# A graph network and expert kernel on one core: update, query and final phases fused by tiles

## The reference, cut to what matters

```python
h = layernorm(x) @ Win.T + b_in
for l in range(3):
    Q, K, V = h @ Wq.T + bq, h @ Wk.T + bk, h @ Wv.T + bv        # 4 heads of 64
    scores = einsum('ehd,egd->ehg', Q[src], K[tgt]) / 8
    msg = einsum('ehg,egd->ehd', softmax(scores), V[tgt]) + Ee[type]
    h = relu(layer_norm(h + segment_sum(msg @ Wo.T + bo, src)) * g + b)
x = x + layernorm(x) + relu(h @ W1.T + b1) @ W2.T + b2
z = layernorm(x); router: 8 logits of z, softmax, the best 2
x = x + weighted sum over the 2 experts: gelu(layernorm(z)*g_e + b_e @ W1_e + b1_e) @ W2_e + b2_e
```

## Time and profile before

| | us |
|---|---|
| median of 3 timed runs | 5030.3 (5026.69 to 5033.61) |
| the profiled execution's own time | 4994.96 |
| its span | 4992.9 |
| mean granted clock of PE | 0.896 |
| PE busy | 3540.9 (71%) |
| DVE busy | 2880.3 (58%) |
| POOL busy | 2496.8 (50%) |
| ACT busy | 1974.2 (40%) |

### The profile page before, as it was taken

One profiled execution on the slowest core, in us unless ns is written; L12 is line 12 of the kernel. 1 busy time (PEld: TensorE's weight loads), 2 busy tenths in 40 slices (PEclk: granted clock), 3 DMA queues, 4 the chain that ended last, 5 costly groups with the idle time before them and its releaser, 6 DMA issues.

```text
span 4992.9 us, 105216 instructions
## 1 busy us (share of the span) xinstructions
PE 3540.9 (71%) x32051; PEld 2742.5 (55%) x32052; DVE 2880.3 (58%) x7542; ACT 1974.2 (40%) x6195; POOL 2496.8 (50%) x2694
## 2 busy tenths in 40 slices
PE   4554066777777786777777777777777778629992
PEld 1113045666666644666666654566666665529991
DVE  7777025777677752777777764377777775620001
ACT  0000044444444445444444443544444444204440
POOL 4787705665666630566665642366666662041113
PEclk9998588999999968999999995899999996659996
DMA  1000034555555523555555542455555552515553
GB/s 27 1 1 6 16 106 128 158 159 156 156 161 160 158 64 131 150 158 159 158 159 159 156 127 87 137 158 160 161 159 160 161 157 82 173 68 185 184 179 111
DMA packets 258168, 640.75 MB, mean 128 GB/s; under 512 B 58336, under 2 KB 121325, under 8 KB 250286
## 3 DMA queue, kind: packets, MB, share of 16 engines
q0 software_dynamic: 161280, 480.04, 33.6%
q1 hardware_dynamic: 96830, 160.07, 9.5%
HBM read 589.52 MB, written 51.00 MB: 128 GB/s over the span
## 4 chain that ended last, share of the span: by engine, by line
PE 34%; DMA 21%; issue 18%; DVE 5%; POOL 4%; another core or an unknown queue 2%; SPq 1%; DVEq 1%; POOLq 1%; ACT 1%; ACTq 0%
DMA arena<-kv_d,gidx 19%; PE bank L1252 7%; PE bank L1242 5%; PE bank L1362 4%; PE bank L1229 4%; PE bank L1374 4%; PE bank L1219 3%; POOL arena L493 2%; PE bank L1235 1%; PE bank L1214 1%; DVE arena L750 1%; POOL tok_d L533 1%; DMA xin<-hid_d 1%; PE bank L1292 1%
## 5 line engine op out<-in xcount | busy, mean ns | idle before, releaser
L493 POOL DMA_INDIRECT arena<-kv_d,gidx x1776 | 1750.8, 986 | 1147.7 <-PE bank L1252 660.9
L1242 PEld LDWEIGHTS bank<-qbd,kt_s 128*128 128x128 f32 x7104 | 979.6, 200 | 55.3 <-ACT kt_s L994 26.4
L709 DVE TENSOR_REDUCE sc<-bank 128x32 f32<-128x512 f32 x888 | 613.7, 691 | 664.9 <-remote 363.4
L1242 PE MATMUL bank<-qbd,kt_s 128*128 128x128 f32 x7104 | 974.8, 282 | 26.7 <-ACT kt_s L994 24.4
L1229 PE MATMUL bank<-ident,arena 128*128 128x128 f32 x3552 | 696.8, 290 | 378.5 <-DMA arena<-kv_d,gidx 350.4
L1252 PE MATMUL bank<-att,arena 128*64 128x64 f32 x14208 | 654.0, 232 | 293.4 <-DVE arena L750 250.0
L1252 PEld LDWEIGHTS bank<-att,arena 128*64 128x64 f32 x14208 | 531.8, 140 | 472.7 <-issue 427.8
L994 ACT ACTIVATE kt_s<-bank 128x512 f32<-128x512 f32 x888 | 521.9, 588 | 581.2 <-PE bank L1229 548.9
L1229 PEld LDWEIGHTS bank<-ident,arena 128*128 128x128 f32 x3552 | 420.5, 145 | 539.6 <-DMA arena<-kv_d,gidx 511.9
L733 DVE TENSOR_TENSOR att<-at_s,arena 128x1024 f32<-128x1024 f32 x444 | 549.1, 1237 | 81.4 <-DVE at_s L730 74.6
L471 POOL DMA_INDIRECT rec_d<-arena x391 | 451.3, 1154 | 175.1 <-issue 126.9
(11 more groups left out here) (205 smaller groups left out, 3857.3 us busy)
## 6 DMA issues: line engine op xcount, KB each, us to landing
arena<-in_pack SPq DMA_DIRECT2D x56, 1030.0 KB, 5.1
arena<-kv_d,gidx POOLq DMA_INDIRECT x1776
xin<-hid_d SPq DMA_DIRECT2D x175, 128.0 KB
kv_d<-arena SPq DMA_DIRECT2D x75, 256.0 KB, 2.0
hid_d<-arena SPq DMA_DIRECT2D x100, 128.0 KB
arena<-in_w SPq DMA_DIRECT2D x4, 2048.0 KB, 9.5
y_d<-arena SPq DMA_DIRECT2D x56, 128.0 KB, 3.7
rec_d<-arena POOLq DMA_INDIRECT x391
```

What stands on the lines that cost most here:

```text
L493: pool.indirect_dma_start(kv[:, t // UB, t % UB, :], None, kv_d, bass.IndirectOffsetOnAxis(gidx[:, h, t - h * HT:t - h * HT + 1], 0),).the ...
L709: dve.tensor_reduce(sc[:, p // 2 % 2, 2 * (p % 2):2 * (p % 2) + 2], bank[p % 4][:, :].rearrange("p (t g s h) -> p t g h s", t=2, g=H, s=W) ...
L1242: ins = mm(bk[:, o:o + P], kt_s[:, p % 2, u, c, :], qbd[:, p % 4, u, :], start=False, stop=(c == KC - 1), skip_group_check=True)
```

## The change

Update and query phase of a layer become one stage, `uq_phase`, that goes by single tiles: in step k each engine does the update of tile k, the statistics of tile k-1, the output of tile k-2, the turning of tile k-3, the products of tile k-4 and the writes of tile k-5, written out without a loop. Update and final phase become `uf_phase` in the same way, over 10 steps of depth. The outer loop over the layers is written out too.

The sums now lie by head (`sums`, 64 rows by 4 heads by nodes): the adds of the edge stage write four runs of 16 numbers, and PE takes them as they lie, four products of 64 rows per tile with Wo cut by heads. The counts are read in place. Neither ACT nor POOL touches the sums or the counts any more. The hidden state no longer goes through `hid_d` to be turned: PE turns it out of `hout` (ACT takes the positive part while it copies). The old state is still read from `hid_d`, by tiles and ahead of time.

In the projection ACT also writes x + layernorm(x) (`xb`, five calls per group, each with a `hold`), SP stores it beside the hidden state and waits for it before it loads the next x; the final stage reads it instead of x. The sums' memset ahead of edge stage 0 moves from POOL to DVE, behind the edge bias `eewo` and ahead of the one-hots (L816); the later ones stay with POOL, behind the last product of the update. `eewo` is made at the end of the query part, by four products. `xnb` is made by POOL out of x1. The logits of all tiles get their bias in one instruction.

DVE in the edge stage:

```diff
                     w = dve.snap(wreg[2 * p + u], min_val=0, max_val=NW - 1)
-                    a = acc[:, ds(w, 1), :].squeeze(1)
-                    dve.tensor_tensor(a, bank[6 + p % 2][u * DH:(u + 1) * DH, 0:DH], a, ALU.add).then_inc(S.chain_a if u == 0 else S.chain_b, 1)
+                    a = sums.rearrange("p h (w s) -> p h w s", s=W)[:, :, ds(w, 1), :].squeeze(2)
+                    dve.tensor_tensor(a,
+                                      bank[6 + p % 2][u * DH:(u + 1) * DH, 0:DH].rearrange("p (s h) -> p h s", h=H),
+                                      a, ALU.add).then_inc(S.chain_a if u == 0 else S.chain_b, 1)
 
                 def turn(i, first):
                     n = l * NTURN + i
```

SP in the fused final stage, from the stores on:

```diff
+                        sp.wait_ge(S.f_x1, n + 1)
+                        sp.dma_start(x1_d[rows(n), :], x1[:, n % G, :]).then_inc(rows_stored[n % G], 16)
+                        if n + G < NT:
+                            sp.dma_start(xo[:, n % G, :], xb_d[rows(n + G), :]).then_inc(xo_landed[n % G], 16)
+                    if k >= 8:
+                        n = k - 8
+                        sp.wait_ge(S.f_xn, n + 1)
+                        sp.dma_start(xn_d[rows(n), :], xnb[:, n % G, :]).then_inc(rows_stored[n % G], 16)
+                    while e < X and w2_after(e) <= k:
+                        sp.wait_ge(S.u_done, at + w2_after(e))
+                        sp.dma_start(w2r[:, e:e + 1], A.w2[:, e:e + 1]).then_inc(S.w2_landed, 16)
+                        e += 1
+
+            for l in range(L - 1):
+                uq_phase(l)
```

POOL, for the tiles of the final stage:

```diff
+            def uf_phase(l):
+                for n in range(NT):
+                    pool.wait_ge(S.f_rs, n + 1)
+                    if n >= G:
+                        pool.wait_ge(rows_stored[n % G], NG * 16 + 32 * (n // G))
+                    pool.tensor_scalar(xnb[:, n % G, :], x1[:, n % G, :], mv[:, 1, n % G, 0:1], rs2[:, n % G, 1:2],
+                                       ALU.subtract, ALU.mult).then_inc(S.f_xn, 1)
+                    pool.wait_ge(S.f_xn, n + 1)
+
```

DVE in the fused update and query stage, and in the fused final stage:

```diff
+            def uq_phase(l):
+                hb = (l + 1) * NT
+                bias(l + 1)
+                for k in range(NT + 5):
+                    if k < NT:
+                        summed(l, k)
+                    if 1 <= k <= NT:
+                        mean(l, k - 1)
+                    if k < NT:
+                        stats(l, k)
+                    if 1 <= k <= NT:
+                        scaled(l, k - 1)
+                    if 2 <= k <= NT + 1:
+                        inverse(l, k - 2)
+                    if k >= 5:
+                        n = k - 5
+                        dve.wait_ge(S.kvp_done, hb + n + 1)
+                        dve.wait_ge(kvo_stored[n % G], 16 + (l + 1) * NG * 16 + (n // G) * 16)
+                        dve.tensor_tensor(kvout[:, n % G, :], bank[6 + n % 2][:, :], bkv[:, :], ALU.add).then_inc(S.kvp_ready, 1)
+                    if 2 <= k <= NT + 1:
+                        shifted_out(l, k - 2)
+                edge_bias(l + 1)
+
+            def uf_phase(l):
+                for k in range(NT + 9):
+                    if 1 <= k <= NT:
+                        mean(l, k - 1)
+                    if 2 <= k <= NT + 1:
+                        inverse(l, k - 2)
+                    if 1 <= k <= NT:
+                        scaled(l, k - 1)
+                    if 6 <= k < NT + 6:
+                        n = k - 6
+                        dve.wait_ge(S.f_adj_done, n + 1)
+                        dve.wait_ge(xo_landed[n % G], (n // G + 1) * 16)
+                        if n >= G:
+                            dve.wait_ge(rows_stored[n % G], NG * 16 + (n // G) * 32)
+                        dve.tensor_tensor(x1[:, n % G, :], bank[3 + n % 3][:, D:2 * D], xo[:, n % G, :], ALU.add).then_inc(S.f_x1, 1)
+                    if 2 <= k <= NT + 1:
+                        shifted_out(l, k - 2)
+                    if 6 <= k < NT + 6:
+                        n = k - 6
+                        dve.wait_ge(S.f_x1, n + 1)
+                        dve.bn_stats(st[:, 1, n % G, :], x1[:, n % G, :]).then_inc(S.f_stat, 1)
+                    if k < NT:
+                        summed(l, k)
+                    if 7 <= k < NT + 7:
+                        n = k - 7
+                        dve.wait_ge(S.f_stat, n + 1)
+                        dve.bn_aggr(mv[:, 1, n % G, :], st[:, 1, n % G, :]).then_inc(S.f_mean, 1)
+                    if 8 <= k < NT + 8:
+                        n = k - 8
+                        dve.wait_ge(S.f_root, n + 1)
+                        dve.reciprocal(rs2[:, n % G, :], sd2[:, n % G, :]).then_inc(S.f_rs, 1)
+                    if k < NT:
+                        stats(l, k)
+                    if 8 <= k < NT + 8:
+                        n = k - 8
+                        dve.wait_ge(S.f_rs, n + 1)
+                        if n >= G:
+                            dve.wait_ge(S.f_zT_done, n - G + 1)
+                        dve.tensor_scalar(zb[:, n % G, :], x1[:, n % G, :], mv[:, 1, n % G, 0:1], rs2[:, n % G, 0:1],
+                                          ALU.subtract, ALU.mult).then_inc(S.f_z, 1)
+
+            bias(0)
```

PE, the same stages:

```diff
+            def update(l, n, ring):
+                dst, at = u_bank(l, n), l * NT + n + 1
+                if n == 0:
+                    pe.wait_ge(S.edges_all, l + 1)
+                if n >= ring:
+                    pe.wait_ge(S.hT_ready, (l + 1) * NT + n - ring + 1)
+                for h in range(H):
+                    mm(dst[:, 0:D], sums[:, h, n * P:(n + 1) * P], wo[:, h, :],
+                       start=(h == 0), stop=False, skip_group_check=True)
+                mm(dst[:, 0:D], cntT[:, n, :], eewo[:, :], start=False, stop=True, skip_group_check=True).then_inc(S.u_done, 1)
+
+            def hidden_turned(l, n):
+                pe.wait_ge(S.hout_ready, (l + 1) * NT + n + 1)
                 for c in range(KC):
-                    ins = mm(bank[7][0:TYPES, 0:D], eeT[:, c, :], wo[:, c, :], start=(c == 0), stop=(c == KC - 1))
-                ins.then_inc(S.ee_done, 1)
...
+            def uq_phase(l):
+                hb = (l + 1) * NT
+                for k in range(NT + 4):
+                    if k < NT:
+                        update(l, k, 4)
+                    if 3 <= k < NT + 3:
+                        hidden_turned(l, k - 3)
+                    if k >= 4:
+                        n = k - 4
+                        if n == 0:
+                            pe.wait_ge(S.wl_landed, q_landed(l + 1))
+                        pe.wait_ge(S.hT_ready, hb + n + 1)
+                        if n >= 2:
+                            pe.wait_ge(S.q_ready, G + hb + n - 1)
+                        queries(bank[4 + n % 2], 0, n % G)
+                        if n >= 2:
+                            pe.wait_ge(S.kvp_ready, 2 + hb + n - 1)
...
+            def uf_phase(l):
+                for k in range(NT + 10):
+                    if 3 <= k < NT + 3:
+                        hidden_turned(l, k - 3)
+                    if 9 <= k < NT + 9:
+                        n = k - 9
...
-
-            q_phase(0)
+                            ins = pe.transpose(bank[6][:, c * P:(c + 1) * P], zb[:, n % G, c * P:(c + 1) * P], ident[:, :])
+                        ins.then_inc(S.f_zT_done, 1)
+                    if 5 <= k < NT + 5:
+                        n = k - 5
+                        pe.wait_ge(S.f_r_ready, n + 1)
+                        mm(bank[3 + n % 3][:, D:2 * D], onesrow[:, :], bf2[0:1, :], start=True, stop=False, skip_group_check=True)
+                        for c in range(KC):
+                            ins = mm(bank[3 + n % 3][:, D:2 * D], rT[:, n % G, c, :], wf2[:, c, :],
+                                     start=False, stop=(c == KC - 1), skip_group_check=True)
+                        ins.then_inc(S.f_adj_done, 1)
+                    if 4 <= k < NT + 4:
+                        n = k - 4
+                        if n == 0:
+                            pe.wait_ge(S.wl_landed, all_landed)
+                        pe.wait_ge(S.hT_ready, (l + 1) * NT + n + 1)
+                        if n >= 3:
+                            pe.wait_ge(S.f_x1, n - 2)
+                        for a in range(KC):
+                            for c in range(KC):
+                                ins = mm(bank[3 + n % 3][:, a * P:(a + 1) * P], wf1[:, c, a * P:(a + 1) * P], xT[:, n % G, c, :],
+                                         start=(c == 0), stop=(c == KC - 1), skip_group_check=True)
+                        ins.then_inc(S.f_u_done, 1)
+                    if k >= 10:
+                        n = k - 10
+                        pe.wait_ge(S.f_zT_ready, n + 1)
+                        for c in range(KC):
+                            ins = mm(bank[7][:, n * X:(n + 1) * X], zT_s[:, n % G, c, :], wr[:, c, :],
+                                     start=(c == 0), stop=(c == KC - 1), skip_group_check=True)
```

(4 more changed lines are left out.)

636 lines of the change are left out of this document (326 added, 310 removed).

## The result

The kernel after takes 5003.9 us (median of 5, 4994.9 to 5009.9), the kernel before on the same chip 5032.7: a ratio of 0.9942, 95% interval 0.9928 to 0.9957. Instead of 126 us the change brings 29. The profiled execution after took 4999.2 us around a span of 4997.4; that of before was 38 us under its own median, that of after 5 us, so the two spans (4992.9 and 4997.4) don't show the gain, and the comparison goes by stages. The sum of this table is not the 29 us: in the two executions that were profiled the changed kernel was 4.5 us longer. Here a stage ends with DVE's last add (edge stages) or its last sum of keys and values, and the final one where the routing starts; an edge stage starts with DVE's first maximum.

The account below looks back on a forecast made before the run. Hand-overs between engines, and the half clock these leave PE with, were taken to bound the update, query and final stages. From the median, 5030.3 us, -110 - 26 + 12 - 2 = -126 gave 4904 us; whole range 4850 to 4990.

Parts of the forecast that it names:

- The clock of the sum: Fused stages: PE instructions priced at full clock, 0.215 us per 256 columns and 0.11 per 128, doubled at half clock.
- a quarter of the 16 be slow: Fused final stage: a quarter of steps 9 to 24 cost 4 to 5 us extra, 17 us more, giving 198.
- half clock: Rival: fused stages stay at 1.2 GHz, update/query 256 us each, final 290, kernel 5230 us; chance 0.08.
- 10 x 0.215: Fused stages: PE's update per tile, five products of 256 columns as ten instructions, 2.15 us.
- The divisor 0.94: Fused update/query: PE's assumed busy share, allowing for more hand-overs; 25 x 4.98 / 0.94 = 132 us.
- At its start the clock is low: I add 6 us: Fused update/query: 6 us for a low clock at the start, within the 139 us forecast per stage.
- 12 us more: Projection: added stores, ACT writes and waits run slowly while GpSimd scatters, 12 us more; bounds 0 and 50.
- Start of edge stage 0, -2: Ahead of edge stage 0: memset moved to DVE delays PE's keys, gathers start earlier; 2 us less, bounds -13 and +12.
- The edge stages. I take 0.: Edge stages: adds writing four runs of 16 and reading PSUM with a step of four cost nothing; bound 90 us.
- Slower adds: Rival: edge-stage adds take longer in the new layout, +90 us, kernel 4994 us; chance 0.05.
- slow code feed: Rival: three stages written out without loops get instructions too slowly, +105 us, kernel 5009 us; chance 0.05.
- The light final loop: Rival: fused final stage's loop is hidden or light, stage 160 us, total -164, kernel 4866 us; chance 0.14.

Follow-up runs that it names:

- late/shallow run: Changed kernel with PE turning zb behind the two products of its step instead of ahead, second product's bias still 1 row deep: 4331.6 us, ratio 0.9803.
- The deep counts in the kernel before: Kernel before with the update's 4-row counts product replaced by one of 128 rows, edges' types and biases left out: ratio 0.9947.
- the two-by-two table: Changed kernel with zb turned early or late, bias product 1 or 128 rows; final stage early 263 and 234.7 us, late 218.5 and 179.0.
- the deep bias: Changed kernel with the second product's bias by a 128-row product instead of 1 row, zb still turned early: 4350.5 us, ratio 0.9827.
- the fill: Changed kernel, zb late, late second weights on ScalarE's queue, 128-row counts product, bias on GpSimd, plus 20 unused products around each edge stage's last four sums: 4221.5 us, 0.9556.
- the 64-row stand-in: Changed kernel with zb turned late and 128-row bias product, its 4-row counts product replaced by one of 64 rows, edges' types and biases left out: ratio 0.9644.
- 128-row counts: Changed kernel, zb late, late second weights on ScalarE's queue, counts product zero-padded to 128 rows: 4890.9 us with 128-row bias product, 4891.5 with bias on GpSimd.

## Why the prediction was wrong

The direction was right, and the size was off by 97 us, outside the range by 14. In the traces the final stage missed its forecast by 56 us and the two fused ones by 29; 10 us that the projection did not lose went the other way. The edge stages, 48 us longer there, can't be set against the medians.

- **"The clock of the sum" and "a quarter of the 16 be slow".** This step failed, for the final stage. It was priced as if PE's waits alone could lower the clock, and only in every fourth step, after a mean of 0.74 in the final stage of before; the rows of the products were in no term. The gap came as worked out (1.5 us where 1.85 stood), PE's step at full clock is 6.05 us (late/shallow run) where 5.2 stood, and the wait behind the weights 7.7 where 13 stood. But the clock was mixed in all steps from step 9 on. Steps 0 to 8 took 53 us (4141.3 to 4194.2) where 32 stood, steps 9 to 24 168 us where 116 + 17 stood, the rest 35 where 20 + 13 stood: 21 + 35 + 2 are the 58 us above 198. At full clock 16 steps of 6.05 + 1.5 would be 121, so the clock cost 47 us there where 17 stood, and most of the 21 at the start. The bound of half clock throughout, 290 us, did not come either: the stage has 255 at a mean of 0.66. The rival "half clock" named the place and had 0.08. Its evidence "stayed at 0.50 for its whole length" stood on the page, and I took its cause to be hand-overs. The deep counts in the kernel before show that it was the 4-row product, which the change moved into all fused stages; the two-by-two table shows that in the final one a new 1-row product and the gap together kept the clock low. The gap too was priced too low: with the deep bias its steps still take 9.3 us. What the gap costs with deep counts as well no run shows.
- **"10 x 0.215" for the update.** Measured 1.92 + 0.62 = 2.54 us, and the transposes behind it 0.37 instead of 0.22 (the prices at each change of depth are below). The divisor 0.94 had covered 0.32 of the 0.54; 25 x 0.22 = 5.5 us per stage.
- **"At its start the clock is low: I add 6 us".** Five updates at half clock, 25.6 us with a 1.2 us wait instead of 12.7, and the first queries: 14 us. The fall lies ahead of the stage, where PE waits for the last turn of the edges; the fill shows it (136.5 us, 2.5 under the 139 forecast). Together these two are the 14 us by which a stage missed 139.
- **Projection "12 us more".** It was 2. The slow instructions beside the scatters did not add up as feared. On the other chips, where SP's five loads take 3.1 us beside the scatters, it was 1 to 2 us too.
- **Start of edge stage 0, -2.** It was 2 us longer, within its bounds.
- **"The edge stages. I take 0."** Right for the adds (223 ns, ratio 1.0003). My own test, "if the edge stages change length by more than 1%", was met by two of the three, and it was a bad test: a single execution of before, 38 us under its median, can't carry it.
- **The rivals.** Slower adds and slow code feed did not come: three straight stages run at the pace of their chain. The light final loop did not come: DVE's way to zb was 1.5 us of the 1.85 assumed, and stayed in the loop.

## What to carry to other kernels

Before a small product is joined to a dense stage, look at the granted clock of the stretch where it ran and at how few rows it has: a bias or a count product of 1 or 4 rows took as much time as a full one here, held one stage at half clock for its whole length and, beside a gap, another below 0.7. Made 128 rows deep with an identity or with zero rows it took no longer (0.62 and 0.63 us). Look also at the clock in the last waits ahead of a stage, and compare stages and medians, not two spans.

## What was not expected of the hardware

A change of depth between two products cost PE time. The chain of waits in the fused stage with the 64-row stand-in (L1415), then with 128-row counts (L1424), each with the transposes behind it:

```profile
1604.00 0.43 PE bank L1415 x2
1604.43 0.37 PE bank L1420 x2
```
```profile
1905.01 0.63 PE bank L1424 x2
1905.64 0.22 PE bank L1429 x2
```

From 64 rows to 64 rows the two take 0.43 us, from 64 to 4 or to 128 rows 0.62 and 0.63; transposes behind 128 rows 0.22, behind 4 or 64 rows 0.37.

Two kinds of chip. On four of six the same kernel takes 4416 instead of 5030 us. Of the 563 us between the spans 4992.9 and 4430.3, 146 lie ahead of the projection's end and 415 in the edge stages, where GpSimd issues transfers. SP's loads of the earlier trace rows on such a chip:

```profile
469.06 3.09 SPq L303 DMA_DIRECT2D xin<-in_x  x5
```

3.1 us where the first chip had 26.6 and 28.0. In the edge stage, 500 us of each, what GpSimd waits for, first chip and second:

```profile
POOL arena L493 <- PE bank L1252: 109.4, 67, 2.0
```
```profile
POOL arena L493 <- PE bank L1252: 7.4, 23, 0.7
```

On the first GpSimd waits 109 of the 500 us for PE's sums (L1252), which free its buffers, on the other 7, and its gathers follow each other at 185 GB/s against 160 inside a stage. In the chain of waits GpSimd's issuing of them has 20.2% there against 3.8%, so I take it to bound the stage. Why the chips differ is open.
